# A loop-closing jump that each engine announces at the top of its round, and the next queries asked for ahead of a batch's keys

## What is computed

```python
x = x + attn(layernorm(x), W_Q, W_K, W_V)
x = x + ffn(layernorm(x), w_gate, w_up, w_down)
# attn: Q = xpos(x @ W_Q); K = xpos(x @ W_K, downscale=True); V = x @ W_V
#       p = softmax(Q K^T) * 0.9 ** |n - m|;  p V
# ffn:  fp4 quantise-dequantise (blocks of 16) of input and weights,
#       silu(gate) * up, the same quantisation again, times w_down
```

## Time and profile before

| what | before |
|---|---|
| median of 3 runs | 2758.21 us (2756.51 to 2759.9) |
| the profiled execution's own time | 2762.61 us |
| its span, first to last instruction | 2760.8 us |
| mean granted TensorE clock | 0.985 |
| PE busy | 2640.3 us (96%) |
| PEld (weight loads, beside PE) | 2364.7 us (86%) |
| DVE, POOL, ACT busy | 80%, 64%, 53% |

### The profile page before, as it was taken

How to read it: one execution, slowest core, us unless ns; L and a number is a source line. 1 busy time by engine, 2 the same in 40 slices (tenths; PEclk the granted TensorE clock), 3 DMA queues, 4 the chain that set the end, 5 groups by cost and what they waited for, 6 DMA issues and landing times.

```text
span 2760.8 us, 52170 instructions
## 1 busy us (share of the span) xinstructions
PE 2640.3 (96%) x16418; PEld 2364.7 (86%) x16418; DVE 2211.2 (80%) x4969; ACT 1465.3 (53%) x2815; POOL 1780.6 (64%) x1563
## 2 busy tenths in 40 slices
PE   7998989999999899999999999999999999999997
PEld 6887779988998789988998889878998899888986
DVE  7999877788878787878788787878777878878785
ACT  6665455555555455555555555545555555555553
POOL 6989946666666566656666666656665665666664
PEclk9999999999999999999999999999999999999999
DMA  7776310021001200031002100120002100210000
GB/s 288 291 271 237 141 40 22 20 83 56 24 18 40 99 22 22 24 103 32 24 20 100 38 22 20 39 96 24 24 24 96 38 24 18 101 40 22 20 24 16
DMA packets 135908, 183.80 MB, mean 67 GB/s; under 512 B 10064, under 2 KB 93136, under 8 KB 135632
## 3 DMA queue, kind: packets, MB, share of 16 engines
q1 hardware_dynamic: 135632, 180.33, 19.0%
HBM read 102.69 MB, written 77.59 MB: 65 GB/s over the span
## 4 chain that ended last, share of the span: by engine, by line
PE 68%; POOL 9%; issue 4%; ACT 3%; DVE 2%; POOLq 0%; ACTq 0%; DVEq 0%
PE score L406 22%; PE acc L525 16%; PE ring L406 15%; PE acc L406 8%; PE ring L498 4%; PE ring L543 3%; POOL probs L831 2%; POOL vals L816 2%; ACT probs L693 2%; POOL h_buf L852 1%; POOL hq_buf L856 1%; DVE smax L1042 1%; DVE xqT L1029 1%; PE ring L490 1%; POOL xv L837 1%
## 5 line engine op out<-in xcount | busy, mean ns | idle before, releaser
L406 PE MATMUL score<-keys,q_st 128*128 128x512 f32 x3072 | 782.9, 404 | 28.0 <-issue 24.3
L831 POOL TENSOR_TENSOR probs<-probs,decay 128x512 f32<-128x512 f32 (+3 forms) x432 | 526.5, 1234 | 432.7 <-ACT probs L693 432.7
L406 PEld LDWEIGHTS score<-keys,q_st 128*128 128x128 f32 x3072 | 570.6, 192 | 147.6 <-issue 30.6
L525 PE MATMUL acc<-vals,pT 128*128 128x256 f32 x4416 | 596.3, 287 | 9.6 <-DVE pT L1029 9.6
L525 PEld LDWEIGHTS acc<-vals,pT 128*128 128x128 f32 x4416 | 558.2, 190 | 24.0 <-issue 9.2
L406 PE MATMUL ring<-w_gu,xqT 128*128 128x512 f32 (+1 forms) x2304 | 510.3, 375 | 0.0
L1042 DVE TENSOR_REDUCE smax<-score 128x1 f32<-128x1024 f32 x256 | 312.9, 1222 | 209.1 <-PE score L406 208.3
L406 PEld LDWEIGHTS ring<-w_gu,xqT 128*128 128x128 f32 x2304 | 419.5, 188 | 63.6
L663 ACT ACTIVATE pT<-ring 128x512 fp32r<-128x512 f32 (+3 forms) x432 | 226.6, 534 | 464.1 <-PE ring L498 456.3
L837 POOL TENSOR_TENSOR xv<-xv,xe 128x256 f32<-128x256 f32 x128 | 94.0, 734 | 434.7 <-DVE xv L910 434.7
L1029 DVE TENSOR_TENSOR pT<-ring,pT 128x512 fp32r<-128x512 f32 (+3 forms) x432 | 251.0, 606 | 72.2 <-ACT pT L663 72.1
(11 more groups left out here) (120 smaller groups left out, 4068.2 us busy)
## 6 DMA issues: line engine op xcount, KB each, us to landing
k_dram<-keys SPq DMA_DIRECT2D x56, 512.0 KB, 4.1
keys<-k_dram SPq DMA_DIRECT2D x56, 512.0 KB, 7.9
q_raw<-q_dram SPq DMA_DIRECT2D x129, 128.0 KB, 2.6
x_in<-X SPq DMA_DIRECT2D x32, 512.0 KB, 4.0
q_dram<-q_stage SPq DMA_DIRECT2D x32, 512.0 KB, 4.9
x_res<-X SPq DMA_DIRECT2D x128, 128.0 KB, 2.0
out<-x_res SPq DMA_DIRECT2D x128, 128.0 KB, 1.7
v_dram<-v_stage SPq DMA_DIRECT2D x28, 512.0 KB, 2.7
```

Source lines behind the costliest of these rows:

```text
L406: mm = pe.matmul(dst, stat(a, k), mov(m, k), start=i == 0, stop=i == n - 1)
L525: mm = pe.matmul(pv_out, pT[g % 2][:, a, j * P:(j + 1) * P], vals[m][:, kb, :], start=i == 0, stop=i == n - 1)
L831: pool.tensor_tensor(probs[:, k0 * P:k1 * P], probs[:, k0 * P:k1 * P], decay[:, off:off + (k1 - k0) * P], ALU.mult).then_inc(decayed, 1)
```

## The change

In SP's `step`, `load_q` is moved ahead of `load_keys`; with that, in step 15 the queries of the next batch's step 1 are asked for in front of its keys. In all other steps the order is unchanged in effect.

```diff
-            with sp.Fori(0, B - 2) as i:
+            with nc.Fori(0, B - 2, engines=bass.OrderedEngineSet([sp.engine]), hint_back_edge=True) as i:
...
             def step(j, s, is_first, more):
+                if s + 2 <= T or more:
+                    load_q(j, s + 2, more)
                 if s == T - 1 and more:
                     for c in range(NC):
                         load_keys(j, c)
-                if s + 2 <= T or more:
-                    load_q(j, s + 2, more)
...
-            with sp.Fori(1, B - 1) as j:
+            with nc.Fori(1, B - 1, engines=bass.OrderedEngineSet([sp.engine]), hint_back_edge=True) as j:
...
-            with pe.Fori(0, LOOPED) as i:
+            with nc.Fori(0, LOOPED, engines=bass.OrderedEngineSet([pe.engine]), hint_back_edge=True) as i:
...
-            with pe.Fori(1, B) as j:
+            with nc.Fori(1, B, engines=bass.OrderedEngineSet([pe.engine]), hint_back_edge=True) as j:
```

More of the change, by code:

```diff
@@ L650, in _ @@
             normalised(0, 1)
-            with act.Fori(0, LOOPED) as i:
+            with nc.Fori(0, LOOPED, engines=bass.OrderedEngineSet([act.engine]), hint_back_edge=True) as i:
                 for c in range(NC):
@@ L737, in _ @@
                 step(first, s)
-            with act.Fori(1, B) as j:
+            with nc.Fori(1, B, engines=bass.OrderedEngineSet([act.engine]), hint_back_edge=True) as j:
                 at = later(j)
@@ L797, in _ @@
                 rstd_chunk(0, c)
-            with pool.Fori(0, LOOPED) as i:
+            with nc.Fori(0, LOOPED, engines=bass.OrderedEngineSet([pool.engine]), hint_back_edge=True) as i:
                 for c in range(NC):
@@ L873, in _ @@
                 step(first, s)
-            with pool.Fori(1, B) as j:
+            with nc.Fori(1, B, engines=bass.OrderedEngineSet([pool.engine]), hint_back_edge=True) as j:
                 at = later(j)
@@ L1017, in _ @@
             chunk_x(0, 0)
-            with dve.Fori(0, LOOPED) as i:
+            with nc.Fori(0, LOOPED, engines=bass.OrderedEngineSet([dve.engine]), hint_back_edge=True) as i:
                 for c in range(NC):
@@ L1168, in _ @@
                 step(first, s)
-            with dve.Fori(1, B) as j:
+            with nc.Fori(1, B, engines=bass.OrderedEngineSet([dve.engine]), hint_back_edge=True) as j:
                 at = later(j)
```

## The result

The changed kernel takes 2724.44 us (median of 4 runs, 2723.85 to 2726.16) against 2758.59 us for the kernel before (4 runs): a ratio of 0.9878, 95% interval 0.9861 to 0.9895, 34 us less. The forecast was 2718 us, with a range of 2712 to 2742.

What follows compares the result with a forecast made beforehand. PE was taken to bound the kernel, with time to gain only at its jumps between batches: 2762.6 - 41.9 + 2 = 2722.7 us for the profiled execution, 2758.2 - 39.9 = 2718 for the median, range 2712 to 2742.

Steps and rivals of the forecast that it cites:

- The seam's price: At each jump back between batches in PE's second loop: standing and low clock cost 6.98 us, six jumps 41.9 us.
- That the target is there in time: PE's second loop: the announced branch falls to a short loop's 0.21 to 0.26 us, saving the whole 41.9 us.
- Run and profiled execution: Last step of the sum: 2722.7 us for the profiled execution, whose time lay 4.4 us above the median, gives 2718.
- The exits: Where PE leaves its two loops and the announcement is wrong: 2 us taken for both, at most 14 us.
- nothing to gain: Loops of POOL, SP and the first stage: jumps already cost 0.2 to 0.3 us, so announcing them saves nothing.
- ACT and DVE: Their second loops: nothing taken; if announcing worked on PE but not DVE, about 1.5 us a seam, 9 us, returns.
- The moved queries: `load_q` ahead of `load_keys` on SP: worth 0 to about 1 us a seam, taken as 0; keys keep 0.4 us slack.
- A: At PE's jumps the target comes too late, requested amid the keys' transfers; half a seam's price stays: 2737 us, chance 0.13.
- B: At the seams the announcement changes nothing, PE's branch stays at 5.8 us: 2758 us, chance 0.10.
- C: Announced target displaces the code that follows: nothing saved at PE's jumps, 7 us lost at each exit: 2772 us, chance 0.07.
- C's sign: A new "issue" wait behind the loop exits at about 164 and 2671 us would show the slower outcome.

## Why the prediction was right

**The seam's price.** Forecast 6.98 us, six times; the changed kernel gives back 6.79, and the kernel written out without PE's jump is as fast as the announced one. That the first instructions had to be brought again is what the code transfers show. Right in mechanism and size.

**That the target is there in time.** Right, but it was taken from the price of a short loop's jump, and it holds on a condition that the prediction did not name: the head's place in its block. With the head at slot 239 the same announcements save 9 us instead of 34. The trace of before had a hint of it that I passed over: at the sixth jump PE stops a second time, 0.17 us, behind 7 score matmuls. That the changed kernel has its head at a good place was luck: nothing in the edit asks for it, and at the other place the time would have been 2750, outside the range. The branch itself takes 0.35 us, not 0.2, and the first register operations of ACT and DVE come 0.5 and 0.6 us behind their branches, not 0.3; neither is seen on PE.

**Run and profiled execution.** The sum was made for the profiled execution: 2722.7 forecast, 2723.85 measured. The error of the median, 2718 against 2724.4, is the step in which I took off 4.4 us because before's profiled execution lay that far above its median. After the change the profiled execution is the fastest of the four runs, 0.6 us below their median. The distance was the scatter of one execution, no constant.

**The exits.** 2 us were taken for PE's two exits. PE's exit from the second loop costs next to nothing: from its branch at 2669.4 to SP's last store takes 0.3 us more than before, though there is one code transfer more, 6.0 us behind the branch. The price, 2.9 us with what else differs, fell on SP, which I had written off with "nothing to gain". The size was about right by luck, for the term was worked out for another engine.

**ACT and DVE.** Their bound was 9 us if only PE were announced; with PE alone and its head placed, 0.5 us a seam is lost, some 3 us. Taking nothing, as they were announced, was right.

**The moved queries.** They were worth 0 to 1 us a seam by the forecast and taken as 0; measured 0 within the error. The keys' slack held: no wait of PE's for them at any seam.

**The rivals.** A was half right. My argument against it, that the announcement is made 299 us ahead, does not count: the transfer that it brings begins only 5 to 6 us before the branch, among the keys' transfers, as A supposed. But that is early enough here. It takes an announcement made 4 us ahead to lose time (2737.6, where I had put 2737; the half in that sum was an assumption, and that it fits this well is chance). B, and with it the sentence of the Trainium skill ("Runtime: NRT & Kernel Launch", section "Instruction fetch mechanics") that prefetch is purely sequential, is refuted here for announced jumps: the same jump lasts 5.8 us unannounced and 0.35 us announced. Its other half, that a jump out of what is held has to wait, was seen at every jump of this loop that was not announced. Of C one part is seen on PE: at the exit the head's block comes in place of the code that follows, which takes one transfer more. But that one comes in time, PE does not stand, and at the taken jumps nothing is lost. Something small of C's kind did cost time or waits elsewhere: code is missing at SP's end, and behind the exits of ACT's and DVE's first-stage loops two new "issue" waits stand, some 20 and 70 us later than C's sign had put them.

## What to carry to other kernels

Look at the loops' own instructions, not only at the busy engines. Here a compare-and-branch of 5.8 us on PE, and gaps of 5.0 and 3.7 us behind those of ACT and DVE, were code that had to be fetched, and a one-instruction announcement at the top of the round cut them to 0.35, 0.5 and 0.6 us. PE sets the end: its one loop alone, announced and well placed, brought 34 us, and ACT's and DVE's another 3. Loops whose jump is already short can be left out: nothing was lost by it, and SP's two announcements went with some 2 us more at the end. Ask for the place of the loop's head in its block of code: a head 17 instructions before a block's end lost three quarters of the gain.

## What was not expected of the hardware

- The place of the loop's head: at the same announcements 2724.4 us at the place that it happened to have, 2750.6 at slot 239; with PE alone announced, 2746.7 where it fell and 2725.4 at slot 0.
- SP, whose jumps take 0.3 us either way, needs 2.5 to 2.7 us from its last branch to its drain wherever its loops were announced, and 0.2 to 0.5 elsewhere, although that branch lies a whole batch behind the loop. Code is fetched in between; why it is missing there is open, and no run separates its two loops.
- An announcement 292 us ahead shows in no transfer until 5 to 6 us before the branch, and one made 3.9 us ahead in a transfer that begins 4.5 to 6.3 us behind it.
- Behind standings of 1.3 to 2.1 us the matmuls of PE's next batch kept their speed (3.04 us for twelve), and behind all of 2.7 us or more the granted clock fell to 0.50 (up to 6 us for twelve). Between these both happened: it stayed at 1.00 behind 2.66 us in the run with PE alone and fell behind 2.17 us at slot 239. Before, where PE stood 3.5 to 4.5 us, the standing was 24.3 of the 41.9 us that six seams cost, and what came behind it 17.6 us.
